# Graph network layer pair: the node blocks' feed-forward and messages inside the attention loop

## What is computed

```python
# layer 0 (h: relu(norm(x)), n = 3125, 8 heads of 32)
q, k, v = split(layernorm(h) @ Wqkv + bqkv)
scores = einsum('ehd,ehd->eh', q[src] * SCALE, k[dst])
e = exp(scores - segment_max(scores, dst)[dst])
agg = segment_sum(v[src] * (e / segment_sum(e, dst)[dst]), dst)
x1 = h + agg
y = layernorm(x1)
y = gelu(y @ W_in + b_in) @ W_out + b_out      # 256 -> 1024 -> 256
x = x + x1 + y
# layer 1
h = relu(norm(x))
h_all = einsum('ni,rio->nro', h, einsum('rb,bio->rio', comp, basis))   # 8 messages of 256 for each node
agg = segment_sum(h_all[src, edge_type], dst)
x = x + layernorm(gelu(agg + h @ loop_w + h_bias + h)) * gamma + beta
```

## Time and profile before

| what | value |
|---|---|
| median of three runs | 1973.73 us (1966.17 to 1980.91) |
| the profiled execution, its own time | 1967.94 us |
| span of its trace | 1966.1 us |
| mean granted clock of PE | 0.822 |
| busy share of the span | PE 66%, PEld 45%, DVE 48%, ACT 20%, POOL 46% |
| set-up | 0 to 145.5 us |
| attention | 145.5 to 868.6 us |
| feed-forward and messages | 868.6 to 1284.0 us |
| relations | 1284.0 to 1966.1 us |

### The profile page before, as it was taken

One profiled execution on the slowest core, in us unless ns is written; L12 is line 12 of the kernel. 1 busy time (PEld: TensorE's weight loads), 2 busy tenths in 40 slices (PEclk: granted clock), 3 DMA queues, 4 the chain that ended last, 5 costly groups with the idle time before them and its releaser, 6 DMA issues. The chain is left out here.

```text
span 1966.1 us, 24864 instructions
## 1 busy us (share of the span) xinstructions
PE 1292.7 (66%) x5024; PEld 882.9 (45%) x5024; DVE 950.3 (48%) x3019; ACT 391.0 (20%) x991; POOL 902.2 (46%) x988
## 2 busy tenths in 40 slices
PE   5766676766676766748999999946534554444542
PEld 3435454555554554535565565524323333333431
DVE  5645565555565655656455452422433433333344
ACT  4542222212222212213323323200000000000000
POOL 3646555555555555532112020156645655555650
PEclk9888888788888888878999999966777777677675
DMA  5566666666666666643211211233333333333331
GB/s 183 143 195 201 190 187 188 178 186 185 178 190 191 177 191 184 182 139 103 107 43 64 107 43 64 86 107 110 104 88 101 101 100 97 96 98 94 104 98 34
DMA packets 136816, 256.53 MB, mean 130 GB/s; under 512 B 39942, under 2 KB 85488, under 8 KB 133586
## 3 DMA queue, kind: packets, MB, share of 16 engines
q0 software_dynamic: 50176, 154.19, 27.4%
q1 hardware_dynamic: 85650, 100.84, 15.6%
q10 hardware_dynamic: 960, 1.18, 0.2%
HBM read 193.49 MB, written 62.65 MB: 130 GB/s over the span
## 5 line engine op out<-in xcount | busy, mean ns | idle before, releaser
L895 POOL DMA_INDIRECT arena<-qv_tab,arena x392 | 393.9, 1005 | 317.1 <-ACT arena L916 166.6
L1497 POOL DMA_INDIRECT arena<-h_all,arena x392 | 374.2, 954 | 278.8 <-DVE arena L1599 165.4
L1566 PE MATMUL ps<-arena 128*128 128x256 f32 x784 | 263.9, 493 | 141.5 <-DMA arena<-h_all,arena 73.9
L999 PE MATMUL ps<-arena 128*128 128x264 f32 x800 | 276.3, 477 | 122.5 <-DVE arena L1078 115.7
L1566 PEld LDWEIGHTS ps<-arena 128*128 128x128 f32 x784 | 186.9, 250 | 211.9 <-DMA arena<-h_all,arena 96.2
L988 PE MATMUL ps<-arena 128*128 128x264 bf16 x1188 | 199.0, 311 | 95.9 <-DVE arena L1067 67.1
L999 PEld LDWEIGHTS ps<-arena 128*128 128x128 f32 x800 | 166.5, 231 | 171.3 <-DVE arena L1078 132.6
L1090 DVE TENSOR_TENSOR arena<-arena,ps 128x512 f32<-128x512 f32 x196 | 134.3, 685 | 204.9 <-remote 101.9
L988 PEld LDWEIGHTS ps<-arena 128*128 128x128 bf16 x1188 | 150.8, 150 | 162.8 <-DVE arena L1067 88.2
L1306 PE MATMUL ps<-wrel,arena 128*128 128x512 f32 x400 | 176.7, 595 | 5.3 <-ACT arena L1246 5.3
L1078 DVE TENSOR_TENSOR arena<-arena 128x512 f32<-128x512 f32 x197 | 134.8, 684 | 92.2 <-ACT arena L942 85.5
(11 more groups left out here) (175 smaller groups left out, 1603.0 us busy)
## 6 DMA issues: line engine op xcount, KB each, us to landing
h_all<-arena SPq DMA_DIRECT2D x25, 1024.0 KB, 3.9
arena<-dst SPq DMA_DIRECT2D x51, 256.0 KB
arena<-k_tab SPq DMA_DIRECT2D x50, 198.0 KB
att<-arena SPq DMA_DIRECT2D x54, 132.0 KB, 5.2
qv_tab<-arena SPq DMA_DIRECT2D x25, 256.0 KB, 3.2
rel<-arena SPq DMA_DIRECT2D x50, 128.0 KB
arena<-qv_tab,arena POOLq DMA_INDIRECT x392, 3.8
arena<-h_all,arena POOLq DMA_INDIRECT x392
```

Source lines behind the costliest of these rows:

```text
L895: pool.indirect_dma_start(out=rowbuf[:, u * T + t, 0:2 * D], out_offset=None, in_=qv_tab, in_offset=bass.IndirectOffsetOnAxis(ap=idx[:, u, ...
L999: last = nc.tensor.matmul(ps[:, 6 + u, 0:AW], ind[:, u, t, :], rowbuf[:, u * T + t, D:2 * D + H], start=(t == 0), stop=False)
L1497: pool.indirect_dma_start(out=rowbuf[:, u * T + t, :], out_offset=None, in_=h_all, in_offset=bass.IndirectOffsetOnAxis(ap=idx[:, u, t:t + ...
L1566: last = nc.tensor.matmul(ps[:, 6 + u, 0:D], ind[:, u, t, :], rowbuf[:, u * T + t, :], start=(t == 0), stop=False)
```

## The change

The middle stage as a block of its own is gone. Its work is in the attention block, one node block m for each pair of visits of the last 22 pairs: the even visit carries its norm and its hidden layers, the odd one (PE's feed stands at the end of the even one) its statistics, Relu and messages. Block 22 begins in the last visit; what is left of it, and blocks 23 and 24, come after it. The buffers of a block are single ones in the arena. The turned indicators share bank 4, the accumulator is bank 5 for all visits, and banks 6 and 7 (BY, BX) serve the node block. Batches of five blocks are gone: each weight tile is now used for 128 columns. ScalarE has all four copies of messages, two table sets in an even visit (Exp and Gelu), and the copy of h1 (before on GpSimd). The inverse square root is now root, with nine small steps, in the relation stage too. The diff is cut; some lines are joined, and remarks on the engine are put behind others.

```diff
+        def root(own, var, h, t, r):
+            own.did(nc.vector.tensor_scalar(h, var, 0.5, 0.5 * EPS, ALU.mult, ALU.add)); own.wait()
+            own.did(nc.vector.tensor_scalar(t.bitcast(I32), h.bitcast(I32), 1, None, ALU.logical_shift_right)); own.wait()
+            own.did(nc.vector.tensor_scalar(r.bitcast(I32), t.bitcast(I32), -1.0, float(HALF_ROOT), ALU.mult, ALU.add)); own.wait()
+            for _ in range(3):
+                own.did(nc.vector.scalar_tensor_tensor(out=t, in0=r, scalar=r, in1=h, op0=ALU.mult, op1=ALU.mult)); own.wait()
+                own.did(nc.vector.scalar_tensor_tensor(out=r, in0=t, scalar=1.5, in1=r, op0=ALU.subtract, op1=ALU.mult)); own.wait()
+            TURN, AGG, BX, BY = 4, 5, 6, 7
...
+                n0 = first_of_both(sp)            # SP; 2 pairs here, the same on each engine
+                with sp.Fori(0, TOGETHER) as m:
+                    v = 2 * (n0 + m)
+                    visit(v, 0)
+                    sp.dma_start(rel[bass.ds(m * P, P), :], zero).then_inc(rel_zeroed, 16)
+                    visit(v + 1, 1)
+                    sp.wait_ge(att_out, 16 * v + 48)
+                    load_block(m + 1)
+                    store_messages(m, 0)          # waits for msg_taken 4 * m + 8
...
+                with pool.Fori(0, TOGETHER - 1) as m:      # GpSimd
+                    visit(2 * (n0 + m) + 2, 0)
+                    visit(2 * (n0 + m) + 3, 1)
+                    residual(m + 1)               # two additions
+                    shift_result(m)               # one
...
+                def visit_hidden(v, u, m):        # ScalarE, even visits
+                    indices(v + 1, 1 - u)
+                    weights(v, u, 0)
+                    take(v - 1, 1 - u)
+                    y_features(m)
+                    weights(v, u, 1)
+                    weights(v, u, 2)
+                    gelu(m, 0)                    # four Gelus of 128 columns
+                    gelu(m, 1)
+                    indicators(v + 1, 1 - u)
+                    weights(v, u, 3)
+                def visit_messages(v, u, m):      # odd visits
+                    indices(v + 1, 1 - u)
+                    weights(v, u, 0)
+                    take(v - 1, 1 - u)
+                    relu(m)
+                    h1_features(m)
+                    weights(v, u, 1)
+                    keep_messages(m, 0)
+                    weights(v, u, 2)
+                    keep_messages(m, 1)
+                    keep_h1(m)
+                    indicators(v + 1, 1 - u)
+                    keep_messages(m, 2)
+                    weights(v, u, 3)
+                    keep_messages(m, 3)
...
+                def message(m, c):                # PE
+                    if c == 0:
+                        pe.wait_ge(h1T_ready, m + 1)
+                    if c >= 2:
+                        pe.wait_ge(msg_taken, 4 * m + c + 3)
                 def across(n, v, u, hid=None, out_of=None):
                     pe.wait_ge(indT_ready, v + 3)
                     keys(n, v, u, 0)
-                    turn(v, u, 0)
-                    turn(v, u, 1)
+                    turn(v, u)
+                    if hid is not None: feed(hid)
+                    if out_of is not None: message(out_of, 2)
                     add_up(v - 1, 1 - u, 2)
                     keys(n, v, u, 1)
                     add_up(v - 1, 1 - u, 3)
+                    if out_of is not None: message(out_of, 3)
                     carry(v - 1, 1 - u)
                 def visit(i, u, hid=None, out_of=None):
+                    if hid is not None: turn_y(hid)
                     keys(i, v, u, 2)
+                    if hid is not None: hidden(hid, 0)
+                    if out_of is not None: turn_h1(out_of); message(out_of, 0)
                     add_up(v, u, 0)
                     keys(i, v, u, 3)
+                    if hid is not None: hidden(hid, 1)
+                    if out_of is not None: message(out_of, 1)
                     add_up(v, u, 1)
                     across(i + u, v + 1, 1 - u, hid, out_of)
...
+                def prepare(m):                   # VectorE, behind the pair j = 0 of an even visit
+                    dve.wait_ge(sums_in, 16 * m + 16)
...
+                def statistics(m):                # behind j = 0 of an odd visit
+                    dve.wait_ge(ff_psum, m + 1)
+                    dve.wait_ge(x_ready, m + 1)
...
+                with dve.Fori(0, TOGETHER) as m:
+                    visit(n0 + m, 0, ahead=m)
+                    visit(n0 + m, 1, behind=m)
-        with nc.Block() as block:                 # the whole middle stage
...
-                    rsqrt(own, vv[:, 0:1], vv[:, 2:3], vv[:, 1:2])      # relations, finish
+                    root(own, zmv[:, 1:2], vv[:, 0:1], vv[:, 1:2], vv[:, 2:3])
```

More of the change, by code:

```diff
@@ L909, in _ @@
                 act.sem_inc(osum_ready, 3)
+                act.sem_inc(h1_ready, 1)
+                act.sem_inc(h1_kept, 1)
+                act.sem_inc(msg_taken, 4)
+                for n in range(2):
+                    act.sem_inc(msg_out[n], 16)
                 with act.If(is_wide(act)):
@@ new lines, in hidden @@
+                def hidden(m, half):
+                    if half == 0:
+                        pe.wait_ge(yT_ready, m + 1)
+                    for n in range(4):
+                        f = 4 * half + n
+                        for k in range(2):
+                            last = nc.tensor.matmul(ps[:, (BY, BX)[half], n * P:(n + 1) * P], win[:, k, f * 128:(f + 1) * 128], yT[:, k, :],
+                                                    start=(k == 0), stop=(k == 1))
+                    last.then_inc(hid_psum, 1)
@@ L1049, in _ @@
                 own.did(nc.vector.memset(osum, 0.0))
+                own.did(nc.vector.memset(zero, 0.0))
                 own.did(nc.vector.memset(sco, 0.0))
@@ L1082, in visit @@
+                BLOCK_STEPS = 3 + 2 + ROOT_STEPS + 2 + ROOT_STEPS
+                def visit(i, u, ahead=None, behind=None):
                     v = 2 * i + u
@@ L1103, in visit @@
                             to_window(i + u, v + 1, 1 - u)
-                with dve.Fori(0, nt) as i:
+                        if j == 0 and ahead is not None:
+                            prepare(ahead)
+                        if j == 0 and behind is not None:
+                            statistics(behind)
+                n0 = first_of_both(dve)
+                with dve.Fori(0, n0) as i:
                     own.loop(i, 2 * 2 * PAIRS)
@@ new lines, in _ @@
+                own.end(n0)
+                with dve.Fori(0, TOGETHER) as m:
+                    own.loop(m, 2 * 2 * PAIRS)
+                    mid.loop(m, BLOCK_STEPS)
+                    visit(n0 + m, 0, ahead=m)
+                    visit(n0 + m, 1, behind=m)
+                own.end(TOGETHER)
+                mid.end(TOGETHER)
+                visit(n0 + TOGETHER, 0, ahead=TOGETHER)
+                shift(PAIRS - 1, own.n)
+                weigh(2 * (n0 + TOGETHER), 0, 3)
+                statistics(TOGETHER)
@@ L1408, in program @@
+                prepare(TOGETHER + 1)
+                for m in range(TOGETHER + 2, NBLK):
+                    prepare(m)
+                    statistics(m - 1)
+                statistics(NBLK - 1)
         with nc.Block() as block:
```

570 lines of the change are left out of this document (261 added, 309 removed).

## The result

The changed kernel takes 2031.9 us in the median (2027.0 to 2035.1), the kernel before 1974.5 beside it: ratio 1.029 (1.025 to 1.034), slower. The profiled execution has a span of 2033.3 us where the sum gave 1917.8: 115.5 more. First the stretches, with the columns of the earlier trace rows: 19 pairs of visits in steady run, what follows the last turn_y of the loop, and the relation stage.

A forecast was written before the change was run, and what follows sets the result against it. The prediction took attention to be bound by a hold behind back-to-back gathers, idling PE 9.0 us a pair. 957.0 plus 22.5 pairs of 42.7 gave 1917.8 us span, 1925 median; own range 1895 to 1950, 8 in 10 1820 to 2055.

The forecast's parts named there:

- the sum: Whole kernel: 957.0 us plus 22.5 pairs of 42.7 gives a span of 1917.8 us.
- the hold: Attention: while gathers run back to back, PE's finished work reaches others only after the batch, 4.5 us a visit.
- the idle 9.0 of a pair: Attention before the change: PE is idle 9.0 us of a 29.2 us pair, as much as the hold.
- PE work of a block: Node block on PE: 15.3 us at the middle stage's clock, plus 0.2 for lower clock; 35.7 busy a pair.
- idle 7: PE in a pair: even visit fills some 3 of 9.0 us, odd none, new handoffs cost 1; 7 stay idle.
- the forecast's 42.7: Attention with the block: a pair takes 42.7 us, PE busy 35.7 plus 7 idle.
- the part on ScalarE: ScalarE in a pair: a block adds 8.5 us, 11 with two table loads; 17.6 in all, no bound.
- The slower rival: Even visit: late Gelu delays feed and the next gathers; pair 48 us, 2045 by the median; chance 0.35.
- Table loads: ScalarE, Exp and Gelu alternating: a switch costs 1.29 us, no drain seen; three loads a pair expected.
- VectorE, GpSimd, SP: Other queues in a pair: VectorE 25 us, GpSimd 22.2, covered; SP's stores and loads free.
- the slow steps: VectorE: a small step that falls under the gathers costs 1.4 us, seven times more.
- Root: Relation stage, 9 steps for 15: 0 under gathers (bound 26 us gain), 3.4 saved in the last three blocks.

The follow-up runs named there:

- x1: Changed kernel with ScalarE's index copy for the even visit's gathers one place earlier, ahead of the fourth message copy: 1878.7 us with the hold, 1633.0 without.
- y3: Changed kernel with Identity in place of Gelu, so without the two table loads a pair: 1592.2 us, on a chip without the hold.
- x3: Kernel before with only the nine-step root in the relation stage's finish: 1945.3 us, 0.986 of the kernel before.
- z3: x1 with both halves of Gelu also ahead of the even visit's third Exp: 1608.6, 1606.7, 1607.7 and 1603.7 us, all without the hold.

## Why the prediction was wrong

In us for a pair, from the windows above and the earlier trace rows (x1 without the hold: turn_y of 21 pairs from 250.19 to 1023.60 in its trace there):

| | with the hold | without | the hold's cost |
|---|---|---|---|
| kernel before | 29.2 | 20.9 | 8.3 |
| changed | 49.4 | 36.8 | 12.6 |
| x1 | 42.1 | 36.8 | 5.3 |

**What bounds the kernel: right, and only half of it.** The hold is there, but it is not the idle 9.0 of a pair: without it 3.9 stay idle (20.9 less 17.0 busy). Its 8.3 are 5.1 of idle time and 3.2 of busy time at the lower clock. That it is absent elsewhere could not be seen in one profile. Without it the kernel before takes 350 us less (1624.1 against 1974.5) and the changed one 403, and there the change moves nothing: 415 us of middle stage go, 22.5 x (36.8 - 20.9) = 358 come back in the pairs, and some 60 as blocks that nothing covers. The block's work is PE's and did not fill the idle time: 3.9 of a pair before, 5.0 after (36.8 less 31.8).

**PE work of a block: the work right, the clock not.** 31.8 busy without the hold, less 2 x 8.5 (325.46/38.25), is 14.8 for a block, against 15.5 in the sum. But "after a hold a whole us at the lower level, 0.50, is seen; I add 0.2 (bound 0 to 3)" was too small. With the hold a pair's busy time is 36.9, 5.1 over that without; the kernel before had 3.2 of these already (20.2 against 17.0). The sum's 35.7 lacks 1.2.

**The step that failed: idle 7.** "Of the 9.0 of hold, the even visit's can be used: PE has the second half of hidden" went by a batch that begins where it did before. The message copies of the change stand ahead of the index copy, the batch starts with the block's work instead of 4 us ahead of it, and its hold covers product, Exp and Gelu: idle 12.5. x1 starts that batch 4.5 us ahead and changes nothing else: 42.05 us a pair. That this is near the forecast's 42.7 is luck in part, since it is made of 8.8 idle and 33.2 busy and not of 7 and 35.7. Without the hold the batch starts level with turn_y too (249.35 and 249.09 in the changed kernel's trace there), and the pair takes 36.8: the place costs only where there is a hold. In the chain of the part on ScalarE ("no bound, but it sits in the chain") the fourth message copy and what waits behind it had no price. Why the first pair has no hold stayed open.

**The slower rival came out in time, and in part by luck.** It gave a pair of 48 and 2045 us. Both of its reasons are seen: Gelu comes after the hold (621.10), and the odd visit's hold lies on turn_h1 to message 0 (3.52). But moving Gelu gave 42 us, and x1, worth 153, leaves the odd visit's hold where it was. What x1 takes away, the start of the even visit's batch behind the fourth message copy, the rival did not name. Accordingly the even visit takes 25.9 us and the odd one 24.1 (keys 2 at 608.85, 634.77 and 658.89), not 22 and 26, and PE waits 1.43 at feed and 3.46 at message 0, not over 4. Still, it alone walked the even visit in order, and at 0.35 its chance was no higher than the forecast's.

**Table loads.** There are two a pair, not three: the one a pair of the kernel before (at L916) is gone. A load at 621.10 lasts 1.28 and Gelu begins at 622.39: 1.29, as in the earlier trace rows. Without the two loads (y3 against the changed kernel, both without the hold, on two chips) 36.6 us go, 1.6 a pair, less than twice 1.28. The drain of 1380 ns that the Trainium skill (ScalarE: Activation LUTs, What ACT_TABLE_LOAD costs) adds to each switch shows in neither.

**VectorE, GpSimd, SP: right, but for the slow steps.** "A step that falls under the gathers costs 1.4" was read from one row and is too wide. The statistics at 631.82 to 633.78 ran in the middle of a batch with 0.19 to 0.25 from step to step, and none of the pairs shown has the slow spacing. GpSimd's additions came behind its gathers, and VectorE never waited for the sums in the loop (once behind it, 5.0 us).

**Root: mis-sized.** "The steps end under the gathers, so 0 there" (3.4 in all) holds without the hold. With it the stage loses 18.7 us between its first and last gather, and x3's median 25.7, close to the bound of 26. Two pairs, of the kernel before and with the root alone, show VectorE's last small steps beside a batch whose first gather began at 1659.84 and 1658.88:

```profile
1670.14 0.16 DVE L1155 TENSOR_TENSOR arena<-arena 128x1 f32<-128x1 f32 x1
...
1673.34 0.16 DVE L1155 TENSOR_TENSOR arena<-arena 128x1 f32<-128x1 f32 x1 [0.59 <-issue]
...
1674.06 0.41 DVE L1639 TENSOR_SCALAR arena<-arena 128x256 f32<-128x256 f32 x1 [0.56 <-DVE arena L1155]
```

```profile
1670.21 0.23 DVE L686 SCALAR_TENSOR_TENSOR arena<-arena 128x1 f32<-128x1 f32 x1
1670.48 0.41 DVE L1654 TENSOR_SCALAR arena<-arena 128x256 f32<-128x256 f32 x1
```

The kernel before has its steps 0.2 us apart up to 1670.14, and the last four take 3.2 us. The nine of root are all 0.19 to 0.25 apart, and the step behind them (L1654 for L1639) comes 11.6 us after the batch's start instead of 14.2. How that gives 0.85 us of a pair was not traced; six steps at 1.4, which would be 8.4 a pair, it is not. The bound was six steps at 0.20, so that x3 came near it by chance. The root is part of the change: less its 25.7 us (x3), the rest of the change is worth some 83 us of loss with the hold, and not 57, an estimate.

## What to carry to other kernels

Work that ran in a stage free of gathers takes on their hold when it is put beside them; price it at the clock and the idle time that the rows beside gathers show, and walk each queue in order, the index copy that starts the next batch first. Where a batch starts against the work can be worth more than the whole change: one instruction, one place earlier, gave 153 us of 2032, and the change cost 57. And a wait that the profile can't name may come and go from chip to chip: x1 is 4.6% under the kernel before with the hold (1.3% of it by the root, x3) and level without it, z3 about 1% under it without. Measure a change like this one where the wait is there and where it is not.

## What was not expected of the hardware

- The same kernel takes 1971 to 1975 us in some sets of runs and 1622 to 1625 in others, on other chips, and within a set it was always one or the other. The difference lies beside gathers: ScalarE's copy follows the start of PE's transposes by 5.8 us in the one and 0.5 in the other, and the 14 traces without the hold have no wait for remote at all. What decides it stayed open.
- The hold has a second price in PE's clock: 0.83 granted in the steady pairs with it, 0.97 without. Keys and message 0, behind 3.43 and 3.46 us of idle PE, ran at 0.50.
- Batches of four gathers, 1.25 us apart, brought about no wait for remote on the chip where most batches of eight did. In the first pair of the changed kernel, and of x1, two batches of eight brought none either.
